# One kernel, the order of its indirect transfers changed: all 32 gathers ahead of all 32 scatters, with smaller first units and the index searches moved between the matmuls

## The reference

```
W   = product of 32 Householder reflections of V          # 128x128
x   = x + W @ layernorm_over_channels(x)
t   = tokens(x)                                           # (4096, 128)
n   = layernorm(t)
S   = softmax(n @ W_router + b_router)                    # (4096, 32 experts)
G, idx = top_k(S.T, 128)                                  # each expert takes its 128 best tokens
tok = n[idx]                                              # (32, 128, 128): the gathers
up  = tok @ W_up[expert // 4] + b_up                      # 8 groups, 341 wide
y_e = silu(up) @ W_down[expert] + b_down                  # 32 experts
y   = zeros.at[idx].add(G * y_e)                          # the scatters, added
out = t + y
```

## Time and profile before

| | |
|---|---|
| median of 3 runs | 212.28 us (211.23 to 212.54) |
| span of the profiled execution, first to last instruction | 210.7 us |
| the profiled execution's own time | not listed apart from its span; the median of the runs stands 1.6 us above the span |
| GpSimd (POOL) busy | 128.0 us, 61% of the span |
| TensorE (PE) busy | 113.5 us, 54% |
| VectorE (DVE) busy | 91.9 us, 44% |
| ScalarE (ACT) busy | 71.0 us, 34% |
| HBM traffic over the span | 130 GB/s |
| DMA queue of the indirect transfers | 4.72 MB, 16.5% of 16 engines |

### The profile page before, as it was taken

One profiled execution on the slowest core, in us unless ns is written; L12 is line 12 of the kernel. 1 busy time (PEld: TensorE's weight loads), 2 busy tenths in 40 slices (PEclk: granted clock), 3 DMA queues, 4 the chain that ended last, 5 costly groups with the idle time before them and its releaser, 6 DMA issues.

```text
span 210.7 us, 2133 instructions
## 1 busy us (share of the span) xinstructions
PE 113.5 (54%) x537; PEld 76.0 (36%) x537; DVE 91.9 (44%) x426; ACT 71.0 (34%) x235; POOL 128.0 (61%) x135
## 2 busy tenths in 40 slices
PE   0699966514221132449999969239259947000390
PEld 0456855401111021123755726037055744000260
DVE  0454998971899886952435405002001202000370
ACT  2148799445544126012242241311213312000161
POOL 2006579886999200677787888878888877750000
PEclk9999999585555555555999999967959988855579
DMA  4999993359999300123233323333333334389898
GB/s 97 295 338 297 290 265 82 85 164 370 239 229 286 104 2 0 31 65 75 64 43 40 44 44 42 54 40 40 47 46 51 40 40 37 26 173 261 228 313 256
DMA packets 43293, 27.62 MB, mean 131 GB/s; under 512 B 6865, under 2 KB 40209, under 8 KB 43281
## 3 DMA queue, kind: packets, MB, share of 16 engines
q1 hardware_dynamic: 36849, 22.75, 39.0%
q0 software_dynamic: 6144, 4.72, 16.5%
q10 hardware_dynamic: 288, 0.03, 0.1%
HBM read 16.48 MB, written 11.01 MB: 130 GB/s over the span
## 4 chain that ended last, share of the span: by engine, by line
PE 23%; POOL 21%; issue 18%; DVE 15%; DMA 14%; ACT 3%; SPq 2%; ACTq 0%; POOLq 0%; DVEq 0%
POOL acc L460 6%; DMA xg<-token_rows,idx 5%; DMA acc<-X,idx 5%; PE PZ L1073 4%; POOL xg L451 4%; PE PT L1061 4%; POOL rs L425 4%; DVE junk L741 3%; PE PM L1061 3%; POOL rs L418 3%; DMA x<-acc 2%; PE PT L913 2%; DMA router_b<-in_L_ffn_b_router 2%; SPq L393 2%; PE PM L1073 2%
## 5 line engine op out<-in xcount | busy, mean ns | idle before, releaser
L460 POOL DMA_INDIRECT acc<-X,idx x32 | 50.2, 1568 | 12.9 <-issue 8.9
L451 POOL DMA_INDIRECT xg<-token_rows,idx x32 | 31.7, 991 | 25.1 <-DVE idx L881 17.8
L892 DVE TENSOR_SCALAR X<-PZ,xg 128x128 f32<-128x128 f32 x22 | 7.7, 351 | 45.4 <-PE PZ L1073 45.4
L1073 PE MATMUL PZ<-wdn,act 128*128 128x128 f32 x132 | 21.1, 307 | 0.9 <-ACT act L570 0.9
L1073 PEld LDWEIGHTS PZ<-wdn,act 128*128 128x128 f32 x132 | 18.5, 215 | 2.7 <-ACT act L570 2.1
L960 PE MATMUL PZ<-stage_w,X 128*128 128x192 f32 x64 | 15.7, 399 | 6.7 <-DVE act L695 6.3
L1050 PE MATMUL PT<-k,xg 128*128 128x128 f32 x32 | 7.0, 352 | 20.7 <-DMA xg<-token_rows,idx 20.7
L1094 PE MATMUL PT<-k,x 128*128 128x128 f32 x32 | 6.7, 373 | 20.5 <-DVE x L897 20.4
L570 ACT ACTIVATE act<-PT,bup 128x512 f32<-128x512 f32 (+3 forms) x14 | 9.0, 640 | 21.8 <-PE PT L1061 21.8
L1061 PE MATMUL PT<-xgT,wup 128*128 128x512 f32 (+3 forms) x28 | 16.2, 665 | 0.0
L960 PEld LDWEIGHTS PZ<-stage_w,X 128*128 128x128 f32 x64 | 13.0, 233 | 8.7 <-DVE act L695 7.9
(11 more groups left out here) (163 smaller groups left out, 248.2 us busy)
## 6 DMA issues: line engine op xcount, KB each, us to landing
X<-in_x SPq DMA_DIRECT2D x8, 256.0 KB, 5.5
acc<-zero SPq DMA_DIRECT2D x4, 512.0 KB, 5.2
acc<-x SPq DMA_DIRECT2D x8, 256.0 KB, 4.2
token_rows<-xf SPq DMA_DIRECT2D x8, 256.0 KB, 3.3
xf<-acc SPq DMA_DIRECT2D x8, 256.0 KB, 5.1
x<-acc SPq DMA_DIRECT2D x8, 256.0 KB, 4.6
out<-X SPq DMA_DIRECT2D x8, 256.0 KB, 3.9
wup<-in_L_ffn_W_up SPq DMA_DIRECT2D x1, 1364.0 KB, 7.9
```

The costliest lines, as they stand in the source:

```text
L451: nc.gpsimd.indirect_dma_start(out=xg[:, e, :], out_offset=None, in_=rows[:, :], in_offset=bass.IndirectOffsetOnAxis(ap=idx[:, e:e + 1], a ...
L460: nc.gpsimd.indirect_dma_start(out=acc[i][:, :], out_offset=bass.IndirectOffsetOnAxis(ap=idx[:, e:e + 1], axis=0), in_=eo[:, e, :], in_off ...
L892: nc.vector.tensor_scalar(eo[:, e, :], down_bank(e), xg[:, e, C + e:C + e + 1], None, ALU.mult).then_inc(s_eo, 1)
L1073: ins = mm(down_bank(e), act[0:rows_, k % 2, j, q * P:(q + 1) * P], w, start=(j == 0), stop=(j == 2))
```

## The change

- GpSimd: `gather(e)` for all 32 experts, then `scatter(e)` for all 32. The constants LEAD and CLOSING go.
- Units: two of two experts first, then seven of four. `gathered_transpose(k + 1)` stands between up(k) and down(k) for every unit.
- Finds: 8 at the start (before: 12, and 4 behind the first transposes); then one ahead of each of the three blocks of up and one ahead of each expert's down, so that 32 are made by the down of expert 11 (before: one behind each down, so that the 32nd comes behind the down of expert 15). VectorE makes the token numbers in the same order, those of a down ahead of that expert's scaling.
- The assignment of scatters to accumulators, the waits of `scatter`, and all behind the last scatter stay.

```diff
-LEAD, CLOSING, AHEAD = 15, 0.77, 16
+FIRST_FINDS = 8
-UNIT_SIZES = (4, 4, 4, 4, 4, 4, 4, 2, 2)
+UNIT_SIZES = (2, 2, 4, 4, 4, 4, 4, 4, 4)
-EARLY = range(1, 9)
+
+def finds_before_up(k, j):
+    e0 = UNITS[k][0]
+    return min(E, FIRST_FINDS + e0 + 3 * k + j + 1)
+
+def finds_before_down(e):
+    k = UNIT_OF[e]
+    return min(E, FIRST_FINDS + e + 3 * (k + 1) + 1)
...
-            gathered = 0
             for e in range(E):
-                while gathered < min(E, LEAD + int(CLOSING * e)):
-                    gather(gathered)
-                    gathered += 1
+                gather(e)
+            for e in range(E):
                 scatter(e)
...
-            for e in range(AHEAD):
-                token_number(e)
-
+            found = 0
             for e in range(E):
+                while found < finds_before_down(e):
+                    token_number(found)
+                    found += 1
                 v.wait_ge(s_dn, e + 1)
                 nc.vector.tensor_scalar(eo[:, e, :], down_bank(e), xg[:, e, C + e:C + e + 1], None, ALU.mult).then_inc(s_eo, 1)
-                token_number(e + AHEAD)
...
-            for e in range(AHEAD - PER):
-                find(e)
+            finds = [0]
+
+            def find_up_to(n):
+                while finds[0] < n:
+                    find(finds[0])
+                    finds[0] += 1
+
+            find_up_to(FIRST_FINDS)
...
                 for j, (f0, fn) in enumerate(FF):
                     at = 3 * k + j
+                    find_up_to(finds_before_up(k, j))
...
                     e = e0 + q
+                    find_up_to(finds_before_down(e))
...
-                    find(e + AHEAD)
...
             gathered_transpose(0)
-            for e in range(AHEAD - PER, AHEAD):
-                find(e)
             for k in range(len(UNITS)):
                 up(k)
-                if k + 1 in EARLY:
+                if k + 1 < len(UNITS):
                     gathered_transpose(k + 1)
                 down(k)
-                if k + 1 not in EARLY and k + 1 < len(UNITS):
-                    gathered_transpose(k + 1)
```

More of the change, by code:

```diff
@@ L874, in token_number @@
             def token_number(e):
-                if e >= E:
-                    return
                 v.wait_ge(s_find, e + 1)
```

## The result

The changed kernel has a median of 217.22 us over four runs (215.15 to 218.37), the kernel before 211.95 us (211.23 to 212.54). The ratio is 1.0229, with a 95% interval of 1.0169 to 1.0289. The forecast was 214.2 us in a range up to 216.2: the direction of the point held, its size did not. (All ratios here are taken within rounds on one chip, and disturbed runs are left out of them, so they need not be the quotient of two medians.)

The account below looks back on a forecast made before the run. GpSimd was taken as the bound: scatter 31 starting at 190.2 instead of 188.13, plus 22.6 us behind it, gives a span of 212.8; with the runs' median above the span, 214.2 us (+0.9%), range 211.4 to 216.2.

Parts of the forecast that it names:

- the price of the order: GpSimd's scatters lose the gathers that hid landings: +3.3 us, less 1.2 us saved on gathers, so scatter 31 starts 2.1 later.
- The step of 4.03 us for two: Scatters alone on GpSimd, each held by the landing of the one two before, go at 4.03 us for two.
- the forecast case: No gather waits for its index, scatters step at 4.03 us for two, scatter 31 starts at 190.2: span 212.8 us.
- The term for the steps: Scatters 0 to 30 on GpSimd are 15 steps of two at 4.03 us, together 60.5 us.
- The same 22.6 us behind it: The work following the start of scatter 31 stays fixed at 22.6 us, as in the kernel before.
- I cost this at nothing; its cover is these 5 us: Finds feeding gathers: the last index comes about 119, gather 31 wants it at 124.4, so late indexes cost nothing.
- The slower rival: Indexes come late for gathers 20 to 31 if TensorE's clock rises later than about 110 us: +5 us, 219; chance 0.08.
- Shorter landings: Rival: without gathers, scatters land sooner and hold 1.87 us each: -2.3 us, 210.0; chance 0.10.
- VectorE in the way of GpSimd: Busy VectorE slows no gather, costed at nothing; a skill rule on the float16 operation would allow up to 1 us.

Follow-up runs that it names:

- b2: The changed kernel with 16 instead of 8 finds ahead of the first transposes, a repeat on another chip: 1.0297 of the kernel before.
- c2: The changed kernel with all 32 finds ahead of the first transposes, so that no gather depends on TensorE's later work: 1.01 of the kernel before.
- d2: The changed kernel with all 32 finds ahead of the first transposes, on another chip: 1.0189 of the kernel before.
- d1: The changed kernel unaltered, run again on a quiet chip: 1.0173 of the kernel before.
- d3: The changed kernel with the units of before, seven of four experts and then two of two: 1.0216 of the kernel before.
- d4: The kernel before with only GpSimd's order changed, all gathers and then all scatters: 1.0353 of the kernel before.
- b3: The changed kernel with scatters over four accumulators, two neither filled nor added, so half of the experts are left out of the output: 1.0122 of the kernel before.
- b4: The changed kernel with GpSimd's mixed order of before put back, 15 gathers and then mixed: 1.0167 of the kernel before.
- a1: The changed kernel with 16 instead of 8 finds ahead of the first transposes: 221.96 us, 1.0289 of the kernel before.
- a2: The kernel before with only GpSimd's order changed, all gathers and then all scatters: 228.01 us, 1.0594 of the kernel before.

## Why the prediction was half right

**What bounds the kernel, and the price of the order: right.** GpSimd stays the bound. The step of 4.03 us for two is 4.02 to 4.10 in every kernel with two accumulators and all gathers first (b2's trace aside), and 3.72 as soon as landings hold nothing up. c2 is the forecast case by itself, span 212.8. By its median it is +1.0%, by d2's +1.9%, with intervals that do not overlap. The term for the steps was 0.8 us short in the first trace and 0.95 in d1; the profiled run of d2 was the fastest of its five (214.39 us, median 215.66), so what made the others longer is in no trace. In the first trace the largest single piece is scatter 9 to 11, 4.58 us, and beside it, at 148.3, lies a load of 16 KB of instructions; d1 has the same pair (5.04 us, the load at 145.9). But d2, d3 and d4 have such a load (149.0, 145.7, 144.7) and no step beside it over 4.12 us, so that the load makes the slip is not shown.

**"The same 22.6 us behind it": not fixed.** The first trace has 21.4, c2 22.2, d1 22.4. In the first trace scatter 31 started 4.48 us after scatter 30 and landed after 5.42 us, where before it was 4.06 and 6.53. That the end was shorter took 1.2 us off and was luck: without it the forecast would have missed by more.

**"I cost this at nothing; its cover is these 5 us": wrong, and this is the step that failed.** It held a rise of the clock at 98 us, from a stage in which unit 0 had four experts. It rose at 111.1, and late indexes, costed at nothing, took 2.9 us. The cover was also worked out for gather 31 alone, and the tightest place is gather 21: with the rise at 105.5 (d1) it waits 0.2 us already, while gather 31 waits for nothing even with the rise at 111.1. Two inputs were off besides. The chain of waits of the changed kernel:

```profile
97.15 1.58 PE PZ L1084 x6
98.72 0.21 PE PZ L1041
98.94 1.15 PE PM L1071 x2
100.09 0.22 PE PZ L1041
```

A block of up for two experts takes 1.15 us at the low level, not half of 1.71, and a down with finds around it 1.58, not the 1.28 of downs in a row. So a unit of two has 3.4 + 3.2 us of up and down and about 8.3 in all, 4.1 for an expert where 3.3 was reckoned. The last find started at 125.0, not at 118.5.

**The slower rival was the right mechanism, but its point comes sooner.** The text put its point at a rise later than about 110 us. At 105.5 (d1) the loss is 0.2 us already, at 111.1 it is 2.9. What was wrong is its chance, 0.08, and that it was set against the forecast where it adds to it. The place was gathers 18 to 21, not 20 to 31.

**Shorter landings: excluded.** Scatters land a median of 3.3 us after their start without gathers as well, and never under 3.2 in the first trace, c2, d1 and d2. The 2.15 us worked out from the page of the Trainium skill, DMA: Bandwidth & Descriptors, section "Anatomy of one DMA — SWDGE (gpsimd) path", did not show; by it b3 could have gained nothing over b1.

**VectorE in the way of GpSimd: not seen.** The other gathers kept 0.94 to 0.96 us. SBUF — State Buffer, section "Who interferes with whom", in the Trainium skill, would have allowed longer ones; no gather in the burst was. The wait went the other way: where the float16 operation (L871, now L878) started 0.50 us or more into a gather, it ended with the gather, within 0.03 us, and took 0.38 to 0.47 us instead of 0.25 (three times in the first trace, twice in d1). That is VectorE's time, at most 0.22 us each.

**The range** reached to 216.2 and left out the late indexes whole. On the quiet chip of d1 the time, 215.6, lies in it; on the first it does not.

## What to carry to other kernels

Two kinds of transfers on one engine may hide each other's latency: before they are sorted by kind, look for the shortest distance between two that depend on each other, and compare it with issue to landing. A producer that feeds such an engine must be costed at the lower clock until a row shows the rise in the same shape of work, and a cover computed from a rise is as uncertain as the rise. It must also be worked out for every transfer that waits, not for the last alone: here the last of 32 had its index in time and four in the middle had not.

## What was not expected of the hardware

Signals of TensorE reached the other engines late, by up to 13.4 us, on two of the chips, while gathers were issued in a row (15 of them in b4). The lags begin 11 to 21 us into the burst and end within 1 to 4 us of its end or of a break in it (a1: last gather issued at 110.3, signals at 113.7; a2: 105.5 and 106.8). The landings of the gathers themselves are not late, 2.2 to 2.7 us to their last packet in a1. The traces of these two chips have 2,567 to 2,816 records of semaphore updates and those of the others 3,112 to 3,120, for the same kernels, so the signals and their records seem to be lost or held together. These runs are all recorded; whether an unrecorded run has such lags, and whether the other cores of a chip take part, stays open. The kernel before was slower on those chips as well (214.6 and 215.0 against 212.2 and 212.4 us), and its own trace there was not taken.

The level of TensorE's clock rose at 105.5, 111.1 and 114.3 us in three traces of one program, at 105.5 and 111.1 in two without late signals, after the same work.
